# First mixture of experts of a four-layer model, weights held in TensorE while 512 tokens stream, with half of the routing-weight products on GpSimd

## What is computed

```python
def body(acc, inp):
    g, u, d, we = inp
    y = jax.nn.silu(x @ g.T) * (x @ u.T) @ d.T
    return (acc + we[:, None] * y, None)
out, _ = jax.lax.scan(body, jnp.zeros_like(x), (gate_proj, up_proj, down_proj, cw.T))
shared = jax.nn.silu(x @ shared_gate.T) * (x @ shared_up.T) @ shared_down.T
return (out + shared).reshape(B, S, H)
```

```python
state = state * dA + (d_t * u_t)[..., None] * B_t[:, None, :]
y_t = jnp.einsum('ben,bn->be', state, C_t)
```

## Time and profile before

| | |
|---|---|
| time of three runs | 1012.67, 1009.87, 1009.8 us; median 1009.87 |
| the profiled execution's own time | 1006.27 us |
| its span, first to last instruction | 1004.5 us |
| PE busy | 821.2 us (82%) |
| DVE busy | 679.0 us (68%) |
| ACT busy | 405.2 us (40%) |
| POOL busy | 419.3 us (42%) |
| mean granted clock of PE | 0.891 |

### The profile page before, as it was taken

The page is one execution under the profiler, slowest core; times in us unless marked ns, Lnnn a source line. Parts: engine busy times, 40 slices in busy tenths (PEclk is TensorE's granted clock), DMA queues, the critical chain, the costliest instruction groups (busy, mean ns, idle before and its releaser), DMA issues.

```text
span 1004.5 us, 12940 instructions
## 1 busy us (share of the span) xinstructions
PE 821.2 (82%) x4202; PEld 521.0 (52%) x4202; DVE 679.0 (68%) x1125; ACT 405.2 (40%) x832; POOL 419.3 (42%) x313
## 2 busy tenths in 40 slices
PE   7968898743988888898389787999975897979993
PEld 3323333332767666676377534555543786546661
DVE  5889999797898888889756645677835546522222
ACT  5843323251444443443254632665540641113331
POOL 3036666012657656665349501414521152323331
PEclk9978887856999999999589997999997998979997
DMA  5121115280212212220200113122026001161114
GB/s 214 48 84 78 68 63 213 121 300 20 84 44 84 83 44 84 84 80 3 73 1 1 39 61 115 51 89 86 28 70 228 9 1 63 43 205 42 49 48 151
DMA packets 28099, 81.68 MB, mean 81 GB/s; under 512 B 3312, under 2 KB 17152, under 8 KB 26528
## 3 DMA queue, kind: packets, MB, share of 16 engines
q1 hardware_dynamic: 25648, 73.25, 21.1%
q0 software_dynamic: 2256, 6.18, 1.7%
q10 hardware_dynamic: 144, 1.57, 0.4%
HBM read 65.64 MB, written 17.35 MB: 83 GB/s over the span
## 4 chain that ended last, share of the span: by engine, by line
PE 41%; DVE 21%; issue 20%; POOL 9%; DMA 4%; ACT 3%; SPq 1%; DVEq 0%; POOLq 0%; ACTq 0%
PE ps L522 6%; POOL M L689 5%; PE ps L1347 5%; PE ps L1714 4%; PE ps L1718 4%; PE ps L513 3%; PE ps L1756 3%; PE ps L911 3%; PE ps L799 2%; POOL ZT L994 2%; PE ps L1366 2%; DVE M L658 2%; DVE M L666 1%; PE ps L1632 1%; PE ps L1364 1%
## 5 line engine op out<-in xcount | busy, mean ns | idle before, releaser
L799 PE MATMUL ps<-W,F 128*128 128x256 f32 x544 | 150.9, 402 | 45.0 <-DVE W L867 22.3
L799 PEld LDWEIGHTS ps<-W,F 128*128 128x128 f32 x544 | 101.7, 197 | 77.9 <-DVE W L867 42.1
L600 POOL TENSOR_TENSOR M<-M 128x1024 f32<-128x1024 f32 x32 | 75.3, 2353 | 86.1 <-DVE M L474 47.4
L696 POOL TENSOR_TENSOR W<-W,M 128x1024 f32<-128x1024 f32 x32 | 75.4, 2355 | 84.5 <-DVE M L666 84.5
L1785 ACT ACTIVATE N<-ps 128x512 f32<-128x512 f32 x128 | 69.5, 595 | 82.2 <-PE ps L1718 82.2
L831 ACT ACTIVATE F<-ps 128x128 f32<-128x128 f32 x136 | 37.7, 277 | 149.8 <-PE ps L799 149.8
L658 DVE TENSOR_TENSOR_SCAN M<-ps,M 128x512 f32<-128x512 f32 x64 | 78.0, 1219 | 21.4 <-POOL M L689 21.4
L1714 PE MATMUL ps<-M,W 32*128 32x256 f32 x512 | 75.4, 424 | 15.8 <-DVE W L1812 10.6
L1806 DVE TENSOR_REDUCE W<-ps 128x4 f32<-128x1024 f32 x64 | 78.1, 1221 | 9.9 <-PE ps L1718 6.8
L786 PE MATMUL ps<-W,F 128*128 128x256 f32 x272 | 83.2, 389 | 0.0
L522 PE MATMUL ps<-M,ident 128*128 128x512 f32 x128 | 74.6, 737 | 7.5 <-DVE M L625 7.5
(11 more groups left out here) (276 smaller groups left out, 1705.6 us busy)
## 6 DMA issues: line engine op xcount, KB each, us to landing
M<-dbl_scratch SPq DMA_DIRECT2D x48, 512.0 KB, 3.8
W<-in_gu SPq DMA_DIRECT2D x1, 4800.0 KB, 16.5
W<-in_gu SPq DMA_DIRECT2D x1, 4352.0 KB, 13.7
att_scratch<-W SPq DMA_DIRECT2D x32, 128.0 KB
slot_scratch<-in_slots SPq DMA_DIRECT2D x1, 3999.0 KB, 18.8
M<-slot_scratch SPq DMA_DIRECT2D x3, 1032.0 KB, 9.3
W<-in_gu SPq DMA_DIRECT2D x2, 1536.0 KB, 7.5
W<-in_dn SPq DMA_DIRECT2D x1, 2176.0 KB, 18.5
```

Source lines behind the costliest of these rows:

```text
L600: nc.gpsimd.tensor_tensor(dBu[:, t, :], du[0][:, t, :], Bb[:, par, :], ALU.mult).then_inc(S("dBu_rdy"), 1)
L696: nc.gpsimd.tensor_tensor(u[1][:, t, :], u[1][:, t, :], hC[:, t, :], ALU.add).then_inc(S("y1_acc"), 1)
L799: last = nc.tensor.matmul(up, ztt[:, par, c, :], gu[:, c, s, :], start=(c == 0), stop=(c == DC - 1))
```

## The change

The experts no longer go by tiles of tokens but by units: for each half of the tokens (512) and each of the 17 units a step k, 34 in all. The unit's weights are held in PE and 512 tokens stream past, so that the hidden values come out with the hidden index on the partitions and need no turning before the down product. The routing weight is then a row along the tokens, no longer a scalar per partition: `cw` is turned once by PE, copied out by ACT, written to DRAM and read back for each step as a row spread over the partitions (`cwb`, three buffers, issued by ACT). The shared expert comes first in each half and has no such weight. The product with the weight is an operation of its own: on DVE on even steps, on POOL on odd ones (`on_pool`), except on steps 17 (the shared expert) and 33. POOL does it ahead of the running sum of the pair whose last piece falls in a later step (`weigh_ahead_of`). The pieces of the scan are dealt out over the 34 steps, 3 or 4 in each (`pieces`). The first half's update and statistics come in steps 17 and 19. Everything is written out, without hardware loops. Three semaphores of the last layer's routing are merged into one, and two of DMAs into another; the later stages are otherwise as before.

The new parts (the DVE, ACT and PE ends of the steps in full):

```diff
+STEPS0 = 2 * FFN[0]["units"]
...
+        def step_unit(k):
+            half, j = divmod(k, 17)
+            return half, j, (j - 1) % 17
+
+        def pieces(k):
+            return range(128 * k // STEPS0, 128 * (k + 1) // STEPS0)
...
+        def on_pool(k):
+            return k % 2 == 1 and k % 17 != 0 and k < STEPS0 - 1
...
+        def stage(q):
+            return next(k for k in range(STEPS0) if 4 * q + 3 in pieces(k))
+
+        def ffn_gpsimd(pool):
             pool.wait_ge(S("cw_done"), 1)
 
+            def weigh_hidden(k):
+                m = weighted(k)
+                pool.wait_ge(S("wide_h"), k + 1)
+                pool.wait_ge(S(f"cw_in{m % 3}"), 16 * (m // 3 + 1))
+                nc.gpsimd.tensor_tensor(h0T[:, k % 2, :], h0T[:, k % 2, :], cwb[:, m % 3, :], ALU.mult).then_inc(S("pool_h"), 1)
+
+            def weigh_ahead_of(q):
+                for k in range(stage(q - 1) if q else 0, stage(q)):
+                    if on_pool(k):
+                        weigh_hidden(k)
+
+            for tile in range(NSTATE // 2):
+                if tile:
+                    weigh_ahead_of(4 * tile - 1)
+                    mamba1_sum(pool, tile - 1, 3)
+                mamba1_drive(pool, tile, 0)
+                mamba1_drive(pool, tile, 1)
+                for k in range(3):
+                    weigh_ahead_of(4 * tile + k)
+                    mamba1_sum(pool, tile, k)
+                    if k < 2:
+                        mamba1_drive(pool, tile, k + 2)
...
+            def gate_up(k):
+                half, _, e = step_unit(k)
+                if k >= 2:
+                    pe.wait_ge(S("wide_h"), k - 1)
+                for part, done in ((0, "wide_gate"), (1, "wide_up")):
                     for c in range(DC):
+                        last = nc.tensor.matmul(ps[:, 4 + 2 * (k % 2) + part, :], gu[:, c, e, part * P:(part + 1) * P],
+                                                ZT[:, c, half * HALF:(half + 1) * HALF], start=(c == 0), stop=(c == DC - 1))
+                    last.then_inc(S(done), 1)
...
+            def down(k):
+                half, j, e = step_unit(k)
+                pe.wait_ge(S("wide_h"), k + 1)
+                if on_pool(k):
+                    pe.wait_ge(S("pool_h"), pool_weighed(k))
...
+                for t in range(4):
+                    last = nc.tensor.matmul(ps[:, 2 + t // 2, (t % 2) * DIM:(t % 2 + 1) * DIM],
+                                            h0T[:, k % 2, t * P:(t + 1) * P], dn[:, e, :], start=(j == 0 and t % 2 == 0),
+                                            stop=(j == 16), skip_group_check=True)
...
+            for k in range(STEPS0):
+                gate_up(k)
+                if k == 1:
+                    weights_turned()
+                if k:
+                    down(k - 1)
+            down(STEPS0 - 1)
...
+            act.dma_start(cw_dram, cwT).then_inc(S("scratch_out"), 16)
+            act.wait_ge(S("scratch_out"), 32)
+            for k in (1, 2):
+                load_weights(k)
+            for k in range(STEPS0):
+                if k + 1 < STEPS0:
+                    tanh(k + 1)
+                if 2 <= k < STEPS0 - 1:
+                    act.wait_ge(S("wide_h"), k - 1)
+                    if pool_weighed(k - 2):
+                        act.wait_ge(S("pool_h"), pool_weighed(k - 2))
+                    load_weights(k + 1)
+                for p in pieces(k):
+                    if p % 4 < 2:
+                        g = p // 4 * 2 + p % 4
+                        if g + 2 < 4 * NSTATE:
+                            mamba1_scalar(act, g + 2)
...
+            def open_gate(k):
+                dve.wait_ge(S("wide_silu"), k + 1)
+                nc.vector.scalar_tensor_tensor(g0T[:, k % 2, :], g0T[:, k % 2, :], 1.0, ps[:, 4 + 2 * (k % 2), :],
+                                               ALU.add, ALU.mult).then_inc(S("silu2_done"), 1)
...
+                up = ps[:, 5 + 2 * (k % 2), :]
+                if k % 17:
+                    done = S("wide_h") if on_pool(k) else S("silu2_done")
+                    nc.vector.tensor_tensor(h0T[:, k % 2, :], g0T[:, k % 2, :], up, ALU.mult).then_inc(done, 1)
...
+            for k in range(STEPS0):
+                mine = list(pieces(k))
+                open_gate(k)
+                mamba1_vector(dve, mine[0])
+                times_up(k)
+                mamba1_vector(dve, mine[1])
+                weigh_hidden(k)
+                if k == 17:
+                    update(0)
+                for p in mine[2:]:
+                    mamba1_vector(dve, p)
+                if k == 19:
+                    dve.wait_ge(S("x_done"), 4)
+                    ln_stats(dve, link, 2, 0)
+            update(1)
```

More of the change, by code:

```diff
@@ L61 @@
 SLOT_LOADS = (2, 5, 8, 8, 8)
+CHOSEN, COUNTS, PLACES, EXPERT_OF = 1, 2, 3, 4
 LD_W3 = 7 * 16
[L63 to L68, removed]
+WIDE_BASE = {1: STEPS0, 2: STEPS0 + 2 * FFN[1]["chunks"]}
 COLS = [("tg", 8), ("freq", 1), ("sign", 1), ("bq3", 1), ("bk3", 1),
@@ L639, in mamba0_vector, with mamba1_vector @@
             weigh_states(NSTATE - 1, 1, False)
[L642 removed]
+        def mamba1_vector(dve, p):
+            tile, j = divmod(p, 16)
             par, t, kind, half = j // 8, (j // 4) % 2, (j % 4) // 2, j % 2
[L645 removed]
             g = (tile * 4 + 2 * par + t) * 2 + half
+            first = tile == 0 and par == 0
             at = slice(half * HALF, (half + 1) * HALF)
[L648 to L651 removed]
             if kind == 0:
@@ L655, in mamba1_vector @@
                     dve.wait_ge(S("dBu1_rdy"), tile * 4 + 2 * par + t + 1)
-                if not start:
+                if not first:
                     dve.wait_ge(S("hC1_rdy"), g - 3)
@@ L666, in mamba1_vector, with mamba1_scalar @@
                 nc.vector.tensor_tensor(hC[:, t, at], hst[:, t, at], Cb[:, par, at], ALU.mult).then_inc(S("hC1_rdy"), 1)
[L668 to L671, removed]
+        def mamba1_scalar(act, g):
+            n, t, half = g // 4, (g // 2) % 2, g % 2
+            if g >= 2:
                 act.wait_ge(S("h1_rdy"), g - 1)
@@ L686, in mamba1_drive @@
                 pool.wait_ge(S(f"bc{par}"), 8 * NSTATE + 32 + tile * 32)
-            if not (isinstance(tile, int) and tile == 0 and par == 0):
+            if not (tile == 0 and par == 0):
                 pool.wait_ge(S("h1_rdy"), (tile * 4 + k - 1) * 2)
@@ L693, in mamba1_sum @@
             pool.wait_ge(S("hC1_rdy"), (tile * 4 + k + 1) * 2)
-            if not (isinstance(tile, int) and tile == 0 and k < 2):
+            if not (tile == 0 and k < 2):
                 pool.wait_ge(S("y1_acc"), tile * 4 + k - 1)
@@ L726, in gu_size @@
             return DC * FFN[f]["units"] * 2 * FFN[f]["width"]
[L728 to L742, removed]
-            pool.wait_ge(S("cw_done"), 1)
[L745 to L754, removed]
-                if f == 0:
-                    if not first:
-                        mamba1_sum(pool, t - 1, 3)
-                    mamba1_drive(pool, t, 0)
-                    mamba1_drive(pool, t, 1)
-                    for k in range(3):
-                        mamba1_sum(pool, t, k)
-                        if k < 2:
-                            mamba1_drive(pool, t, k + 2)
-            tiles(pool, body, (lambda t: mamba1_sum(pool, t, 3)) if f == 0 else (lambda t: None))
@@ L1188, in route_tensor @@
             nc.tensor.matmul(ps[:, 1, 0:n_te], every, upto, start=False, stop=True)
-            nc.tensor.matmul(ps[:, 0, 0:NEXP], every, upto[:, NT - 1, :], start=True, stop=True).then_inc(S("counts"), 1)
+            nc.tensor.matmul(ps[:, 0, 0:NEXP], every, upto[:, NT - 1, :], start=True, stop=True).then_inc(S("routed"), 1)
         def route_places(dve, link):
@@ L2123, in _ @@
             router_vector(dve, link, 0)
-            ffn_vector(dve, 0, link)
-            for half in range(2):
-                ln_stats(dve, link, 2, half)
+            ffn_vector(dve, link)
             ln_apply(dve, 2)
```

236 lines of the change are left out of this document (95 added, 141 removed).

## The result

The change made the kernel slower: 1032.97 us (median of 4 runs, 1029.26 to 1035.09) against 1011.27 (4 runs, 1009.8 to 1013.09), a ratio of 1.0205, 95% interval 1.0171 to 1.0239. The profiled execution took 1033.23 us, against 1006.27 before, so the two profiles differ by 27.0 us where the medians differ by 21.7.

A forecast was written before the change was run, and what follows sets the result against it. The prediction took a loop of POOL and VectorE, not TensorE, as the bound. Stage +11.3, end -0.8 and clock +3 gave +13.5 us on 1006.3 us profiled, 3.6 below the median: 1023 us, own range 1013 to 1031, wide range 1000 to 1036.

The forecast's parts named there:

- rival 3: TensorE becomes the stage's bound at a clock of 0.76: +16 us in place of 3, 1036 us; chance 0.13.
- What bounds the kernel: In the rewritten stage, POOL's sums and drives and VectorE's products form a loop, 6.48 us from sum to sum.
- The late gate: Gate matmul queued behind the down group awaiting POOL's routing-weight product delays VectorE's gate opening by 0.9 to 3 us.
- the walk: Stepping through POOL's and VectorE's queues with predicted instruction prices; it gave tiles of 30.1 to 33.4 us, the stage +11.3 us.
- From W to the gate: From the routing-weight product's end to VectorE's gate opening: down 1.73, gate 1.72, tanh 0.60, semaphores 0.25, so 4.3 us.
- Clock: TensorE, idle at late products, clocks lower and lengthens the way to the gate: 1.1 to 4.9 us, taken as 3.
- POOL's exposed products: Routing-weight products on POOL that lengthen the stage's loop: 16 at 0.9 us, 14 us.
- Start and end: First sum 9.0 us after weights ready, next tile's opening sum at 28.6; end 7.0 us against 7.8, so -0.8.
- The stage: From weights ready to the last sum's start: 246.5 us against 235.2, so +11.3 us, before 3 us for the clock.
- The port: VectorE products with two SBUF operands stand until POOL's instruction ends; by this lock alone the stage holds 217 us, before 187.
- The faster one: POOL's products fit its idle time, no gate late: 995 us at full effect, 1002 at a little over half; chance 0.27.
- The bound by TensorE's clock: Same as rival 3: TensorE's 175 us of work needs 230 us at clock 0.76; 1036 us, chance 0.13.

The follow-up runs named there:

- e11: Kernel before, with POOL's sums and drives alternating evenly over the tiles' edges too: 996.83 us, ratio 0.9831.
- e1: Changed kernel with TensorE's down groups two steps late and the first half's update one step later, POOL's products kept: 1009.46 us, ratio 0.999.
- e3: Changed kernel with the step's gate and up matmuls repeated ahead of each TensorE wait for POOL's product: 1024.41 us (1 run).
- e7: Changed kernel without the routing-weight products and their row loads, with down groups two steps late: 990.61 us (1 run).
- e6: Changed kernel with down groups two steps late and all 32 routing-weight products on VectorE: 1013.12 us, ratio 0.9979.
- e8: Changed kernel with down groups two steps late, all products on VectorE, and POOL's sums and drives alternating over tile edges: 992.87 us, ratio 0.9783.
- e10: Changed kernel with down groups two steps late and POOL's sums and drives alternating over tile edges, POOL's 15 products kept: 997.87 us, ratio 0.987.
- e2: Changed kernel with all 32 routing-weight products on VectorE, TensorE's order kept: 1017.96 us (1 run).

## Why the prediction was right, and where its sum was not

The forecast was 1023 us in a range of 1000 to 1036, slower at 0.65; it is slower, at 1033.0. The direction and its cause were right and the size was short: +13.5 us on the profiled execution were forecast and 27.0 measured, 9.0 of the difference in the stage and 5.1 behind it. The time lies 2 us outside the forecast's own range of 1013 to 1031, and nearer to rival 3's 1036 than to 1023; it is the wide range that took it in. Point by point:

1. **What bounds the kernel: held, and one row was under-read.** The loop of POOL and VectorE carries the stage. But the 21.4 us that the scans waited for D were taken as given; e11 shows that 18.5 us of the kernel before hung on the order of the drives at the tiles' edges.
2. **The late gate: right mechanism, and the term of the sum that failed.** I wrote: "In the walk it holds G7 by 0.9, G11 by 2.0, G15 by 2.5, G25, G27, G29, G31 by 1 to 2.5 and G33 by 3", 8 places and 12 to 18 us of waiting, and worth 10.5 us of the stage, 13.5 with the clock. Measured: 42.2 us of waiting, worth 25.3 us (after against e1). All eight places came true, at 2.6 to 5.1 us each where the walk had 0.9 to 3. G13, G17 and G23 came on top with 2.4, 2.4 and 1.6 us, and nine short waits with 4.8 us together.
3. **From W to the gate** I had 4.3 us, and 0.6 more by the clock. At full clock that price holds (4.49 at two places, 4.43 at six of e3), but nine of the eleven took 6.0 to 6.5. The place shown above took 6.2: the down group 3.5 from start to start at 1.2 GHz in place of 1.73, the gate's half 1.9 in place of 1.72.
4. **Clock:** I took +3 us. Keeping it up (e3) gave 11.3 back. My mistake was to spread the mean clock of a stage, 0.85, over the chain: the chain from W to G is just where TensorE comes out of its idle spell, so at most places it ran at the lower level there, whatever the mean. The mean, 0.89, came out as forecast, and so did TensorE's busy time (200 expected, 195.9 measured); neither told of this.
5. **POOL's exposed products: near, a little over-priced.** I had 16 of them (there are 15: the odd steps up to 31 but for 17) at some 0.9 us, 14 us. On the path all 32 products cost 22.1 us with POOL's among them (e1 against e7) and 21.5 with all on VectorE (e6 against e7). If each costs the same, POOL's 15 come to some 10 us; that is an estimate, no run separates them. What would have been saved by VectorE doing them is 0.6 us (e1 against e6). The walk without its late gates had a stage of 246.5 - 10.5 = 236.0 us, and e1 measures 232.7. So the sum's two errors in the stage are 11.8 us too little for late gates and clock (13.5 for 25.3) and 3.3 us too much for the rest.
6. **Start and end: near.** The first sum was to start 9.0 us after the weights were ready, and started 7.7 us after the first drive; S3 at 28.6, measured 27.0; tail 7.0, measured 7.2. The tiles were to take 30.8, 30.1, 30.2, 32.5, 30.3, 30.6 and 33.4 us and took 31.6, 32.3, 32.1, 32.1, 31.8, 34.2 and 36.9: late gates in every one, and most in the last two.
7. **The stage:** 246.5 + 3, measured 258.0. With the clock kept up (e3) it is 246.7. That this is the walk's figure is luck: late gates without the clock's part are 246.7 - 232.7 = 14.0 us where the walk had 10.5, and the rest is the 3.3 us less of point 5.
8. **The port** behaved as the rows of before said, on the new instructions too: W on VectorE took 0.67 us free and up to 2.83 behind a POOL instruction.
9. **The rivals.** The faster one needed "no G waits"; e1 makes that true, and the stage is 232.7, not the 222 to 229 that it gave: with the gates on time the products still lie on the path (point 5), on POOL as much as on VectorE. POOL's idle time did not swallow them. The bound by TensorE's clock did not come true as put (a clock of 0.76 all through), but its mechanism did at the places that matter: nine of the ways from W to the gate were run by TensorE at the lower level, where the rival had some 15.

What the streaming of 512 tokens is worth without the faults: with the even order and all products on VectorE the stage takes 217.9 us (e8), with the old tiling 216.2 (e11). It takes 136 x 0.57 = 78 us of small units off VectorE, puts 34 x 1.22 = 41 us of G and T there, and a product that costs 21 us on the path; TensorE, which it relieves (208.4 us busy in e11, 182.6 in e8), was not what the stage waited for. Whether e8 or e11 is the faster of the two is open: their ratios to before overlap, and they ran on different chips.

Not tried: POOL's product ahead of the drive instead of ahead of the sum, and a routing weight that needs no product of its own. That the 5.9 us of e10 are the port's is argued from the longer instructions, not shown by a run.

## What to carry to other kernels

Before an operation is moved to an engine with idle time, ask what is queued behind the instruction that waits for it. Here an idle POOL delayed one matmul group, and the next step's first matmul stood behind that; ordering the group a step later (e1) gave the whole loss back at no cost. Such a chain starts after an idle spell, so look up in a trace what it takes at TensorE's lower level, and don't go by the mean clock of the stage. An engine's idle time doesn't make the work moved there free: here it cost as much on POOL as on VectorE. And look at the order at the seams of a loop first: a few exchanged instructions in the kernel before (e11, 0.983) were worth more than this rewriting without its late gates (e6, 0.998).

## What the runs showed of the hardware

- Most down groups behind several microseconds of idle time ran at 1.2 GHz (3.64 us for 1.89 behind 4.67 us); behind 1.06 us it was 1.99. The length of the idle spell alone doesn't tell it, though: in e1 the group behind 5.11 us took 3.75 us and the one behind 2.41 us 1.97, but one behind 3.40 us took 1.97 and one behind 1.93 us 3.06.

TensorE in order of time, e1_down_two_late:

```profile
344.62 3.75 PE L780 MATMUL ps<-W 128*128 128x256 f32 x8 [5.11 <-POOL W L731]
...
397.07 1.97 PE L780 MATMUL ps<-W 128*128 128x256 f32 x8 [2.41 <-POOL W L731]
...
412.09 1.97 PE L780 MATMUL ps<-W 128*128 128x256 f32 x8 [3.40 <-POOL W L731]
...
440.30 3.06 PE L780 MATMUL ps<-W 128*128 128x256 f32 x8 [1.93 <-POOL W L731]
```

- The wait goes both ways. In the change VectorE's h started at 252.07, inside a drive that ended at 254.04, and ended at 254.58, so 0.54 us behind it; POOL's product, started at 254.00, took 1.71 us where 7 of the 15 took 1.26 or 1.27. The drive took up to 2.80 in place of 2.34. The Trainium skill (SBUF — State Buffer, section Who interferes with whom) has an exclusive lock there, where the later one stands until the first is done, and these rows agree.
- The part of the kernel that no edit touched differed by up to 14 us between profiles (525.1 to 539.1), while the stages of e1, e2 and e6 agreed within 1 us. A difference in one execution's total of a few microseconds says nothing here; the stage does.
